# Moving the weighted sum of two expert rows from VectorE to GpSimd in a two-layer attention and expert kernel

## The reference, cut to what matters

```
xn = layernorm(x);  x = x + attention0(xn) + experts0(xn)
xn = layernorm(x);  x = x + attention1(xn) + experts1(xn)
```

```
multiplier, selected = sparsemixer_eval(x @ router_w.T)     # two shares, two experts
out = sum over e of dense_w[:, e] * ((silu(x @ w_gate[e].T) * (x @ w_up[e].T)) @ w_down[e].T)
```

## Time and profile before

| | |
|---|---|
| median of three executions | 2558.47 us (2558.06 to 2561.96) |
| the profiled execution, its own time | 2557.68 us |
| its span (first to last instruction) | 2555.9 us |
| PE busy | 2315.6 us, 91% |
| DVE busy | 1982.7 us, 78% |
| ACT busy | 1660.5 us, 65% |
| POOL busy | 737.2 us, 29% |
| mean granted TensorE clock | 0.962 |

### The profile page before, as it was taken

The page is one execution under the profiler, slowest core; times in us unless marked ns, Lnnn a source line. Parts: engine busy times, 40 slices in busy tenths (PEclk is TensorE's granted clock), DMA queues, the critical chain, the costliest instruction groups (busy, mean ns, idle before and its releaser), DMA issues.

```text
span 2555.9 us, 64898 instructions
## 1 busy us (share of the span) xinstructions
PE 2315.6 (91%) x25503; PEld 1656.1 (65%) x25503; DVE 1982.7 (78%) x3435; ACT 1660.5 (65%) x3050; POOL 737.2 (29%) x621
## 2 busy tenths in 40 slices
PE   6989989899898998989989899898998989988998
PEld 3667566665666666766667666676666766666665
DVE  6778877788778887787876878868778687786986
ACT  4866558665686656775567755767457684585845
POOL 2220432205322052221522215212253023530234
PEclk8999999999999999999989999999999999999999
DMA  7110211103111121111211112111121112211022
GB/s 250 51 42 2 106 54 43 42 19 104 39 45 39 43 84 35 47 38 43 88 32 49 34 47 88 33 48 30 63 76 34 44 30 76 68 35 49 19 78 63
DMA packets 99124, 141.35 MB, mean 55 GB/s; under 512 B 11523, under 2 KB 60620, under 8 KB 98316
## 3 DMA queue, kind: packets, MB, share of 16 engines
q1 hardware_dynamic: 90636, 120.41, 14.9%
q0 software_dynamic: 8192, 16.79, 2.3%
HBM read 101.84 MB, written 31.13 MB: 52 GB/s over the span
## 4 chain that ended last, share of the span: by engine, by line
PE 60%; DVE 20%; issue 10%; ACT 8%; POOL 1%; SPq 0%; DVEq 0%; DMA 0%; ACTq 0%; POOLq 0%
PE ps L1552 11%; PE ps L1723 7%; DVE neg_max L1209 7%; PE ps L1745 6%; PE ps L1760 6%; PE ps L1559 6%; PE ps L1634 5%; ACT probs L821 4%; PE ps L1656 3%; PE ps L1509 2%; DVE ffn L1352 2%; PE ps L1573 2%; DVE probsT L1219 2%; DVE key_low L977 2%; PE ps L1645 1%
## 5 line engine op out<-in xcount | busy, mean ns | idle before, releaser
L1209 DVE TENSOR_REDUCE neg_max<-ps 128x1 f32<-128x1024 f32 x512 | 622.2, 1216 | 85.9 <-PE ps L1723 79.3
L821 ACT ACTIVATE probs<-ps,neg_max 128x1024 f32<-128x1024 f32 x512 | 577.0, 1127 | 76.1 <-DVE neg_max L1209 72.8
L1552 PE MATMUL ps<-shared,w_split 128*128 128x512 f32 x1536 | 471.1, 443 | 18.2 <-ACT ffn L872 11.6
L1745 PEld LDWEIGHTS ps<-ident,probs 64*128 64x128 f32 x8192 | 338.4, 145 | 172.3 <-issue 134.7
L706 POOL TENSOR_TENSOR probs<-ffn,shared 128x512 f32<-128x512 f32 x208 | 287.7, 1383 | 410.6 <-DVE ffn L1352 183.4
L1745 PE MATMUL ps<-ident,probs 64*128 64x64 f32 x8192 | 364.7, 231 | 41.4 <-issue 28.5
L1552 PEld LDWEIGHTS ps<-shared,w_split 128*128 128x128 f32 x1536 | 288.9, 193 | 165.0 <-issue 62.9
L872 ACT ACTIVATE ffn<-ps,room_of_gate 128x512 f32<-128x512 f32 x256 | 175.0, 683 | 270.5 <-PE ps L1552 270.5
L1723 PE MATMUL ps<-shared,query_a 64*128 64x512 f32 x1024 | 268.6, 521 | 84.5 <-ACT probs L821 62.2
L1760 PE MATMUL ps<-probsT,latent 128*32 128x128 f32 x8192 | 327.0, 279 | 12.9 <-DVE o_latent L1202 12.7
L805 ACT COPY probsT<-ps 128x512 f32<-128x512 f32 x512 | 303.2, 592 | 25.8 <-PE ps L1745 24.3
(11 more groups left out here) (231 smaller groups left out, 3501.7 us busy)
## 6 DMA issues: line engine op xcount, KB each, us to landing
w_split<-w_parts SPq DMA_DIRECT2D x132, 256.0 KB, 2.6
shared<-gate_rows SPq DMA_DIRECT2D x64, 512.0 KB, 4.4
y_rows<-probs SPq DMA_DIRECT2D x40, 256.0 KB, 2.2
x_in<-in_x SPq DMA_DIRECT2D x9, 512.0 KB, 4.1
out<-x_mid SPq DMA_DIRECT2D x8, 512.0 KB, 3.2
ffn<-in_gate_up SPq DMA_DIRECT2D x1, 2048.0 KB, 8.7
probsT<-in_gate_up SPq DMA_DIRECT2D x1, 2048.0 KB, 13.4
w_down<-in_down SPq DMA_DIRECT2D x2, 1024.0 KB
```

The source lines that it names most:

```text
L821: nc.scalar.activation(probs[:, t % 3, :], banks(2 * (t % 2)), ACT.Exp, bias=neg_max[:, t % 4:t % 4 + 1], accum_out=row_sum[:, g % 2, t % ...
L1209: nc.vector.tensor_reduce(neg_max[:, t % 4:t % 4 + 1], banks(2 * (t % 2)), X, ALU.max, negate=True).then_inc(max_ready.sem, 1)
L1552: mm = nc.tensor.matmul(ps[:, bank, :], w_split[:, f % CHUNK_SLOTS, h, k * P:(k + 1) * P], tokens[:, half], start=(part == 0), stop=(part ...
L1745: mm = nc.tensor.transpose(ps[:, turn_bank(t, c), k * HQ:(k + 1) * HQ], probs[rows, t % 3, k * P:(k + 1) * P], ident[rows, rows])
```

## The change

DVE's 16 steps go. POOL gets four operations over all tokens behind the gathers: two multiplications in place, `y_pair[:, k] *= share_k` (128 x 1024 each, the share spread over 128 columns by a step of zero), then two additions to `x_mid` (128 x 1024 each). It waits for the shares (a new semaphore `shares_ready`, raised by the last reciprocal on DVE, which DVE itself no longer waits for), for all four groups of gathers, and for its own operations between one another.

```diff
-COMBINE_STEP = PERIOD + 16
-DVE_STEPS = 58
+DVE_STEPS = 57
@@ semaphores
-        combined = signal("combined", 2 * NT)
+        shares_ready = signal("shares_ready", 1)
+        combined = signal("combined", 4)
@@ gpsimd, behind the gathers and ahead of inverse_deviation(b, 2, ...)
+                pool.wait_ge(shares_ready.sem, shares_ready.at(b, 1))
+                for part in gathered:
+                    pool.wait_ge(part.sem, part.at(b, 16 * 2 * NT // GATHERS))
+                for k, share in enumerate((r_s1, r_s2)):
+                    nc.gpsimd.tensor_tensor(y_pair[:, k, :, :], y_pair[:, k, :, :],
+                                            share[:, :].unsqueeze(2).to_broadcast([P, NT, D]), ALU.mult
+                                            ).then_inc(combined.sem, 1)
+                pool.wait_ge(x_taken.sem, x_taken.at(b, 1))
+                for k in range(2):
+                    pool.wait_ge(combined.sem, combined.at(b, 2 + k))
+                    nc.gpsimd.tensor_tensor(x_mid[:, :, :], x_mid[:, :, :], y_pair[:, k, :, :], ALU.add
+                                            ).then_inc(combined.sem, 1)
@@ vector, route_weights
-                        link(nc.vector.reciprocal(total[:, :], total[:, :]))
+                        inverse = nc.vector.reciprocal(total[:, :], total[:, :])
+                        if k == 1:
+                            inverse.then_inc(shares_ready.sem, 1)
+                        else:
+                            link(inverse)
@@ vector, attention_step
-                    if COMBINE_STEP <= w < COMBINE_STEP + 2 * NT:
-                        n, choice = divmod(w - COMBINE_STEP, 2)
-                        if choice == 0:
-                            dve.wait_ge(x_taken.sem, x_taken.at(b, 1))
-                            dve.wait_ge(gathered[n * GATHERS // NT].sem,
-                                        gathered[n * GATHERS // NT].at(b, 16 * 2 * NT // GATHERS))
-                        else:
-                            dve.wait_ge(combined.sem, combined.at(b, 2 * n + 1))
-                        nc.vector.scalar_tensor_tensor(x_mid[:, n, :], y_pair[:, choice, n, :],
-                                                       (r_s1, r_s2)[choice][:, n:n + 1], x_mid[:, n, :],
-                                                       ALU.mult, ALU.add).then_inc(combined.sem, 1)
@@ vector, before the first add of the output projection
-                            dve.wait_ge(combined.sem, combined.at(b, 2 * NT))
+                            dve.wait_ge(combined.sem, combined.at(b, 4))
```

## The result

The changed kernel took 2539.81 us (median of six runs, 2534.90 to 2547.04); the kernel before took 2559.65 us in the same comparison. The ratio is 0.9924, with a 95% interval of [0.9911, 0.9937]: 19.8 us faster. The forecast was 2528.1 us with a range of 2524.5 to 2538.0. The sign was right; the gain is two thirds of the forecast, and the time lies 1.8 us above the range. The profiled execution took 2537.11 us with a span of 2535.4 us.

The account below looks back on a forecast made before the run. DVE was taken to bound the second attention run's sixteen steps with most sums. Saving 3.8 us a sequence, 30.4 in all, from the profiled 2557.68 gave 2527.3; plus 0.8 for the median, 2528.1 us, range 2524.5 to 2538.

Parts of the forecast that it names:

- The bound and the price of a sum: Second attention run, sixteen steps holding most sums: DVE is the limit, and each sum costs 0.26 us of its queue.
- Part 1: Second attention run without DVE's sums: groups of four steps at 7.15 us; 3.8 us saved a sequence, 30.4 in all.
- Rival A: Second attention run paced worse than its best four steps: 7.44 us a group, 21 us saved, 2537 us; chance 0.15.
- The tail: End of the second attention run, from PE's last mark to the last maximum: another 0.72 us saved a sequence.
- The prediction's own sign of being wrong: Second run less than 2.9 us shorter, or the stretch between the runs or behind them longer.
- Parts 2 and 3: POOL's sum behind the gathers: 8.7 us a sequence, hidden by 29 us of cover, costing DVE beside it nothing.
- Rival C: POOL holds DVE's maxima and copies in the second run: 4.9 us worse a sequence, 2597 us; chance 0.03.
- The wider reading: DVE beside POOL: their shared write interface, read widely, would hold copies into SBUF; the mechanism of rival C.

## Why the prediction was wrong, step by step

**The bound and the price of a sum: right.** DVE bounded the sixteen steps. Putting the same operations back takes the whole gain away, and the groups that POOL doesn't touch return to 7.9 and 8.2 us.

**Part 1, the pace: the step that failed.** "At 7.15 each, four groups take 28.6 us." They take 29.17 in the last sequence, at a granted clock of 1.00. The 7.15 was read from one group, and its neighbour, at 7.44, was explained away: "those four steps already contain sums". They do, but that is not why it is long. ACT makes one copy more in every second group, and with the sums gone that is what bounds the group. The row that could have shown it was there: ACT busy 6.87 of 7.15 in the short group, and one more copy takes 816.28 - 815.82 = 0.46 us of its queue, which makes 7.33 of the 7.44 (the 0.46 is read in the changed kernel, but the same copy stood in the one before). I counted the saved copy for DVE and never charged it to ACT. Rival A was nearer (7.44 for every group, where the mean is 7.29; 2537 us), but for a vague reason and with a chance of only 0.15.

**The tail: mis-sized, for the same reason.** From the last mark to the projection it went from 2425.70 - 2418.29 = 7.41 to 2402.44 - 2395.49 = 6.95 us: 0.46 where the term was 0.72. ACT's fourth double copy of the run lies beside that last mark; in the last sequence of the kernel without double copies the tail is 6.72 us. With the pace that makes 31.76 - 29.17 + 0.46 = 3.05 us in this sequence, and 24.3 us for eight over the whole stretch from the first gather to the projection, which takes 501.6 us in all before and 477.2 after. The forecast had 30.4; this accounts for 6 us of the 10.6 that are missing between the two medians. Part 1's sum is in effect that of the kernel without double copies: in its last sequence the sixteen steps take 28.69 us, so that they and the tail are 31.76 - 28.69 + 7.41 - 6.72 = 3.76 us shorter, and the whole stretch, at 469.8 us, is 31.8 us shorter in eight. The prediction's own sign of being wrong, a second run less than 2.9 us shorter, did not appear (24.3 us are 3.04 a sequence). With the pace and the tail as measured and nothing else changed, the time would have been 2558.47 - 24.3 = 2534.2 us, inside the range; what took it out of the range is what follows.

**Parts 2 and 3, POOL: right.** 1.90 us for a multiplication (2.0 forecast), about 2.4 for an addition (2.36), hidden with 29 us to spare, and nobody held. Rival C fell by three runs: the sum left out, the work doubled, and the collision that holds only the operation with two SBUF inputs. The wider reading that the prediction gave to rival C, by which copies into SBUF would be held as well, is not borne out by any of them.

**What no part of the sum had: the TensorE clock.** Each of these three stretches goes from a projection to the next sequence's first scatter, and has the same work (x1049 on PE). The first is of the kernel before, the others of the changed one (columns as in the earlier trace rows, the granted clock third from the end; its two levels are 1.2 and 2.4 GHz, so 0.93 means more time at the lower):

```profile
2114.60:2276.95 162.35, 149.47 (x1049) 102.83 (x1046) 126.59 (x207) 92.52 (x148) 59.12 (x42) 0.96 0.20 63
```

```profile
228.74:396.14 167.40, 153.67 (x1049) 105.89 (x1046) 127.89 (x207) 92.43 (x148) 58.05 (x41) 0.93 0.20 61
2093.63:2256.53 162.90, 149.88 (x1049) 102.78 (x1046) 127.14 (x207) 92.42 (x148) 58.08 (x41) 0.96 0.19 63
```

Both kernels show 162 to 167 us for it, longer where the clock is lower; the seven stretches sum to 1152.6 us before and 1151.7 after, so the change does not lengthen them. The profiled executions differ in the last stretch, from the last projection to the end: 130.20 us at a clock of 0.97 before, 132.96 at 0.94 after. Over all runs whose clock was listed, the kernel before has a mean of 0.962 and 2560.6 us (43 runs), the changed one 0.960 and 2539.4 us (12). At one clock, 0.962, the kernel before has a mean of 2559.9 us (five runs) and the changed one 2534.9 (five): 25.0 us; at 0.960 it is 21.7 us (eight runs and two). One straight line of time on clock for each kernel, with the same slope, fitted to all 55 runs, puts 24.0 us between them at equal clock (standard error 0.9), which agrees with the 24.3 of the marks, and 2.8 us on the difference of the clocks. So by this estimate some 3 us of the missing gain go with a lower granted clock; the last 1 to 2 us are a matter of which runs fell into the comparison. That time and clock go together is shown; why the kernels without sums get the lower clock more often is open, and no run here tries it. A kernel that is shorter by 3 us in each of eight sequences may meet the changes of clock elsewhere; that is only a guess.

## What to carry to other kernels

When one engine of a nearly balanced loop is relieved, work out the load of every engine for every step of its pattern, and charge each moved instruction to the engine that has it; a floor read from one period holds for that period's share of the pattern alone. An assignment made to relieve an engine (here ACT's extra copies) should be tried again once that engine is relieved in another way: undoing it took 7 us off here, and the kernel with the other run balanced by place was another 10 us faster, of which the groups show about half. Elementwise work with much slack before its deadline is well placed on GpSimd, if nothing with two SBUF inputs is left on DVE beside it.

## What the runs showed of the hardware

- A DVE operation of 128 x 128 with two SBUF inputs took up to 2.53 us beside a GpSimd addition and 0.34 without; maxima and copies from PSUM beside 8.6 to 18 us of GpSimd work kept 1.22 and 0.68 us.
- GpSimd multiplies 128 x 1024 float32 by a share spread with a step of zero in 1.90 us and adds two full tiles in about 2.4 us.
- The same products (some 250 records) at the head of the first attention run took 24.42 us at a granted clock of 0.86, 25.15 at 0.80 and 26.46 at 0.74, all in one execution (the kernel with the second run's copies on DVE).
- Twelve executions of the changed kernel spread over 13 us with the mean granted clock: 2534 to 2537 us at 0.962, 2544 to 2547 at 0.956 or 0.957. The clock is not all of it: eight executions of the kernel before at 0.960 took 2560.33 to 2568.49 us. I had not expected a difference of 0.005 in the mean clock to be worth 10 us, half of what the change gains.
